# Four graph layers on one core: spline index blocks staged two ahead, rank picks half a block later, packed label products, aligned loops

## The reference

```python
# layer 0, twice: spline convolution, mean over incoming edges
msg = (1 - u) * (x @ w[0])[src] + u * (x @ w[1])[src]
h = segment_sum(msg, dst) / max(degree, 1) + x @ root + bias
# layer 1: opinion attention; edge_label is 8 wide, trans_weight 8 x 64
ef = edge_label @ trans_weight
att = sigmoid(leaky(x[row] * x[col] @ a) + leaky(ef @ edge_attention_weight))
# for values ef*att, x[col]*att, x[row]*att: segment sum, mean and max by row and by col
out = concat(...) @ weight + bias
# layer 2: three GCN convolutions; layer 3: softmax attention over incoming edges
```

## Time and profile before

| | us |
|---|---|
| median of three runs | 20658.94 |
| lowest, highest | 20649.24, 20679.84 |
| the profiled execution, its own time | 20593.66 |
| its span in the profile | 20591.8 |
| POOL busy | 12080.9 (59%) |
| DVE busy | 8998.8 (44%) |
| PE busy, its weight loads | 7375.4 (36%), 6283.1 |
| ACT busy | 2698.1 (13%) |

### The profile page before, as it was taken

How to read it: one execution, slowest core, us unless ns; L and a number is a source line. 1 busy time by engine, 2 the same in 40 slices (tenths; PEclk the granted TensorE clock), 3 DMA queues, 4 the chain that set the end, 5 groups by cost and what they waited for, 6 DMA issues and landing times. The chain is left out here.

```text
span 20591.8 us, 194797 instructions
## 1 busy us (share of the span) xinstructions
PE 7375.4 (36%) x49884; PEld 6283.1 (31%) x49884; DVE 8998.8 (44%) x25746; ACT 2698.1 (13%) x7499; POOL 12080.9 (59%) x11797
## 2 busy tenths in 40 slices
PE   3444444444322232232244544434444444400000
PEld 2333333333232232233211444434443333300000
DVE  3554533333343343344388444444443444333333
ACT  1222212222100000000023111111110111000000
POOL 4666656566566666666611466666665665466664
PEclk9655555555555555555555677767776666555555
DMA  1222212222122222222266000000000000022221
GB/s 56 62 62 62 63 58 80 80 82 84 59 86 81 79 83 84 79 82 81 82 222 234 8 11 12 11 11 11 12 11 19 22 21 21 15 55 56 57 56 42
DMA packets 599140, 1231.22 MB, mean 60 GB/s; under 512 B 229172, under 2 KB 351769, under 8 KB 572838
## 3 DMA queue, kind: packets, MB, share of 16 engines
q0 software_dynamic: 378560, 479.32, 10.7%
q1 hardware_dynamic: 206420, 692.77, 9.3%
q10 hardware_dynamic: 14112, 58.61, 0.8%
HBM read 560.63 MB, written 669.21 MB: 60 GB/s over the span
## 5 line engine op out<-in xcount | busy, mean ns | idle before, releaser
L795 POOL DMA_INDIRECT rows<-gcn_table,index x3430 | 3746.6, 1092 | 2491.0 <-ACT index L803 1509.6
L516 POOL DMA_INDIRECT rows<-spline_table,index x3136 | 3231.6, 1030 | 2038.5 <-ACT index L534 1077.5
L850 PE MATMUL p_slots<-part,lo_t 128*128 128x208 bf16 x18816 | 2549.3, 300 | 2920.8 <-ACT lo_t L812 1809.8
L850 PEld LDWEIGHTS p_slots<-part,lo_t 128*128 128x128 bf16 x18816 | 2007.1, 116 | 3346.1 <-issue 2369.6
L1036 POOL DMA_INDIRECT sent<-a_msg,a_place x1568 | 1578.1, 1006 | 1186.2 <-DVE a_run L1151 712.9
L1378 POOL DMA_INDIRECT e_rows<-soft_table,e_index x1568 | 1520.8, 970 | 845.3 <-issue 491.8
L1028 POOL DMA_INDIRECT a_rows<-att_table,a_index x1568 | 1506.5, 961 | 484.6 <-issue 470.4
L868 DVE TENSOR_TENSOR one_lo<-iota,lo 128x2560 bf16<-128x2560 f32 (+1 forms) x297 | 733.3, 2469 | 2315.5 <-ACT index L803 2125.4
L1092 PE MATMUL a_p_label<-tw,a_label 8*128 8x64 f32 x3136 | 1000.5, 401 | 2036.4 <-issue 1481.1
L1092 PEld LDWEIGHTS a_p_label<-tw,a_label 8*128 8x128 f32 x3136 | 853.2, 318 | 2014.7 <-issue 1728.4
L812 ACT ACTIVATE lo_t<-p_turn 128x512 bf16<-128x512 bf16 x1287 | 719.4, 595 | 5130.8 <-remote 3495.3
(11 more groups left out here) (398 smaller groups left out, 16071.2 us busy)
## 6 DMA issues: line engine op xcount, KB each, us to landing
running_dst<-a_run SPq DMA_DIRECT2D x98, 1600.0 KB
running_src<-s_run SPq DMA_DIRECT2D x98, 1600.0 KB
running<-e_run SPq DMA_DIRECT2D x98, 656.0 KB
s_rows<-sent ACTq DMA_DIRECT2D x98, 584.0 KB
rows<-gcn_table,index POOLq DMA_INDIRECT x3430
running<-run SPq DMA_DIRECT2D x98, 520.0 KB
rows<-spline_table,index POOLq DMA_INDIRECT x3136
running<-run SPq DMA_DIRECT2D x98, 512.0 KB
```

Source lines behind the costliest of these rows:

```text
L516: pool.indirect_dma_start(out=rows[h][:, k, :], out_offset=None, in_=table, in_offset=offsets(index[h][:, k:k + 1])).then_inc(gathered[h], 16)
L795: pool.indirect_dma_start(out=rows[h][:, ON_CHIP + k, :], out_offset=None, in_=table, in_offset=offsets(index[h][:, k:k + 1])).then_inc(ga ...
L850: ins = nc.tensor.matmul(p_slots[:, m, 0:CLASS * SLICE], lo_t[h][:, k, q, :], flat(part[:, c, q * CLASS:(q + 1) * CLASS, :]), start=q == 0 ...
```

## The change

It has three parts.

1. **Spline passes.** Indices are staged two halves ahead: ACT copies those of half n + 2 once the gathers of half n have landed, ahead of `stage` and the rank chain; the first two blocks are staged before the loop. POOL gets a wait for the messages of the half two back (step `MADE` = 2), since nothing else now keeps it from overwriting rows. Pick and reduction of half n − 1 move to half n, after the running chain and ahead of the one-hots; `p_look` is doubled for it. DVE's first iteration stands ahead of the loop, a memset counts two steps for the pick that is left out there, and the last pick follows the loop.
2. **Attention pass.** The labels are loaded packed: `a_label` is 128 partitions (16 columns × 8 labels) by 128 edges, 512 B a row of the DMA. PE makes one score product (16 columns wide) and two label products of 512 columns a half with the block-diagonal `w_labels`, in place of 32 small products. `tw_att` becomes the matching 128 × 16 block-diagonal vector, made once by a copy, a wider product and a reduction; the load of `tw` goes.
3. **Every pass, every engine:** `addr_align(256)` ahead of the loop puts its first instruction at a multiple of 256 in the engine's program, by empty instructions ahead of it.

```diff
@@ -483,11 +483,12 @@
...
             p_same = ctx.enter_context(nc.psum_tensor(f"p_same{uid}", [P, 12, P], F32))
-            p_look = ctx.enter_context(nc.psum_tensor(f"p_look{uid}", [P, RANKED, C], F32))
+            p_look = ctx.enter_context(nc.psum_tensor(f"p_look{uid}", [P, 2, RANKED, C], F32))
             turned, turned_sb, same, same_sb, summed, seen_sb, looked = (sem(n) for n in ("turned", "turned_sb", "same", "same_sb", "summed", "seen_sb", "looked"))
...
         running_v = running[0:EP, :].rearrange("(p t) c -> p t c", p=P)
-        INIT = per
+        INIT = 2 * per
+        MADE = 2
         Q = RANKED // GROUP
@@ -495,6 +496,7 @@
...
                 sp.dma_start(running[EP:EP + 1, cut], zeros[0:1, cut]).then_inc(stored[h], 16)
+            sp.addr_align(256)
             with sp.Fori(0, IT) as i:
@@ -507,10 +509,13 @@
...
         def _(pool):
+            pool.addr_align(256)
             with pool.Fori(0, IT) as i:
...
                     pool.wait_ge(indexed[h], i + 1)
+
+                    pool.wait_ge(stepped, INIT + per * (2 * i + h - 2) + MADE)
                     pool.sem_inc(sig["rounds"].sem, 1)
@@ -552,13 +557,15 @@
...
             stage_index(0, 0)
+            stage_index(1, B)
             stage(0, 0)
+            act.addr_align(256)
             with act.Fori(0, IT) as i:
...
-                    act.wait_ge(stepped, INIT + per * n - (per - 2))
-                    stage_index(1 - h, (n + 1) * B)
+                    act.wait_ge(gathered[h], 16 * B * (i + 1))
+                    stage_index(h, (n + 2) * B)
@@ -618,11 +625,12 @@
...
                             kk = q * GROUP + k
-                            nc.tensor.matmul(p_look[:, kk, 0:J], lo_tf[q % 2][:, k, :], seen[q % 2][:], start=True, stop=False)
+                            nc.tensor.matmul(p_look[:, h, kk, 0:J], lo_tf[q % 2][:, k, :], seen[q % 2][:], start=True, stop=False)
                             for j in range(k + 1):
-                                ins = nc.tensor.matmul(p_look[:, kk, 0:J], earlier[q % 2][:, PAIR[j] + k - j, :], one_hi[h][:, q * GROUP + j, :], start=False, stop=j == k)
+                                ins = nc.tensor.matmul(p_look[:, h, kk, 0:J], earlier[q % 2][:, PAIR[j] + k - j, :], one_hi[h][:, q * GROUP + j, :], start=False, stop=j == k)
                         ins.then_inc(looked, 1)
+                pe.addr_align(256)
                 with pe.Fori(0, IT) as i:
@@ -653,47 +661,68 @@
...
                 one_hots(0, lambda ins: ins.then_inc(stepped, 1))
-            with dve.Fori(0, IT) as i:
+            def pick(h, half, step):
+                dve.wait_ge(looked, Q * half)
+                step(nc.vector.tensor_tensor(picked[:], p_look[:, h, :, 0:J], one_hi[h][:], ALU.mult))
+
+            def rank_of(at, step):
+                step(nc.vector.tensor_reduce(edge["rank"][:, at], picked[:], AX.X, ALU.add))
+
+            def both_halves(i, first):
                 for h in range(2):
...
-                    def step(ins):
-                        ins.then_inc(stepped, 1)
-                        n[0] += 1
+                    def step(ins, by=1):
+                        ins.then_inc(stepped, by)
+                        n[0] += by
...
+                    half = 2 * i + h
                     dve.wait_ge(staged[h], i + 1)
...
                     step(nc.vector.tensor_tensor(msg[h][:, :, 0:C], msg[h][:, :, 0:C], rows[h][:, :, 0:C], ALU.add))
+                    assert n[0] == MADE
...
                         step(nc.vector.scalar_tensor_tensor(run[h][:, k, :], before, keep[h][:, k:k + 1], msg[h][:, k, :], ALU.mult, ALU.add))
+                    skipped = rank and first and h == 0
+                    if rank and not skipped:
+
+                        pick(1 - h, half, step)
+                        after()
+                        rank_of(bass.ds((half - 1) * B + ranked, RANKED), step)
                     if count or rank:
...
-                        dve.wait_ge(counted, 1 + B * (2 * i + h))
+                        dve.wait_ge(counted, 1 + B * half)
                     if count or rank:
                         one_hots(1 - h, step)
-                    if rank:
-
-                        dve.wait_ge(looked, Q * (2 * i + h + 1))
-                        step(nc.vector.tensor_tensor(picked[:], p_look[:, :, 0:J], one_hi[h][:], ALU.mult))
-                        after()
-                        step(nc.vector.tensor_reduce(edge["rank"][:, bass.ds((2 * i + h) * B + ranked, RANKED)], picked[:], AX.X, ALU.add))
+                    if skipped:
+                        step(nc.vector.memset(picked[:], 0.0), 2)
                     assert n[0] == per
-            dve.wait_ge(stepped, INIT + per * 2 * IT)
+            both_halves(0, True)
+            dve.addr_align(256)
+            with dve.Fori(1, IT) as i:
+                both_halves(i, False)
+            if rank:
+                done = lambda ins, by=1: ins.then_inc(stepped, by)
+                dve.wait_ge(stepped, INIT + per * 2 * IT)
+                pick(1, 2 * IT, done)
+                dve.wait_ge(stepped, INIT + per * 2 * IT + 1)
+                rank_of(slice((2 * IT - 1) * B + ranked, (2 * IT - 1) * B + B // 2 + ranked), done)
+            dve.wait_ge(stepped, INIT + per * 2 * IT + 2 * rank)
             nc.vector.tensor_copy(final[:, 0:width], run[1][:, B - 1, :]).then_inc(stepped, 1)
@@ -974,7 +1008,7 @@
...
         begun, xdst = pair("a_begun", [P, B, C]), pair("a_xdst", [P, B, C])
-        label, label_row = pair("a_label", [LABELS, B * P]), pair("a_label_row", [P, B, LABELS])
+        label, label_row = pair("a_label", [B * LABELS, P]), pair("a_label_row", [P, B, LABELS])
         product = sb("a_product", [P, B, C])
@@ -989,12 +1023,14 @@
...
         PLACED = 1 + B + 11
+        PRODUCTS = B * C // 512
...
                 sp.dma_start(begun[h][:], node_rows_v[:, bass.ds(n * B, B), :]).then_inc(loaded[h], 16)
-                sp.dma_start(label[h][:], labels[:, bass.ds(n * (B * P), B * P)]).then_inc(loaded[h], 16)
+                packed = labels[:, bass.ds(n * (B * P), B * P)].rearrange("l (k p) -> k l p", p=P)
+                sp.dma_start(label[h][:], packed).then_inc(loaded[h], 16)
                 sp.dma_start(label_row[h][:], label_rows[:, bass.ds(n * B, B), :]).then_inc(loaded[h], 16)
@@ -1081,16 +1120,17 @@
...
         def _(pe):
+            pe.addr_align(256)
             with pe.Fori(0, IT) as i:
...
                     pe.wait_ge(stepped, INIT + per * (2 * i + h - 1))
-                    for k in range(B):
-                        edges = label[h][:, k * P:(k + 1) * P]
-                        nc.tensor.matmul(p_label[h][:, k, :], edges, w_label, start=True, stop=True)
-                        ins = nc.tensor.matmul(p_score[h][:, k:k + 1], edges, w_label_att, start=True, stop=True)
+                    nc.tensor.matmul(p_score[h][:, 0:B], label[h][:], w_label_att, start=True, stop=True)
+                    for m in range(PRODUCTS):
+                        cut = slice(m * B // PRODUCTS, (m + 1) * B // PRODUCTS)
+                        ins = nc.tensor.matmul(flat(p_label[h][:, cut, :]), label[h][:], flat(w_labels[:, cut, :]), start=True, stop=True)
                     ins.then_inc(labelled, 1)
@@ -1654,7 +1704,7 @@
...
         w_ef, w_lab, twt = sb("w_ef", [C, 2, C]), sb("w_lab", [2 * LABELS, C]), sb("twt", [C, 3 * LABELS])
-        tw, ea, tw_att = sb("tw", [LABELS, C]), sb("ea", [C, 1]), sb("tw_att", [LABELS, 1])
+        ea, tw_att, tw_rows = sb("ea", [C, 1]), sb("tw_att", [B * LABELS, B]), sb("tw_rows", [C, B, LABELS])
         w_labels = sb("w_labels", [B * LABELS, B, C])
@@ -1665,7 +1715,7 @@
...
             (w_src[:], w_att[0:2 * C, :]), (w_dst[:], w_att[2 * C:4 * C, :]), (w_ef[:, 0, :], w_att[C:2 * C, :]), (w_ef[:, 1, :], w_att[3 * C:4 * C, :]),
-            (b1[:], bias1.broadcast_to([P, C])), (tw[:], trans), (twt[:, 0:LABELS], trans_t), (twt[:, LABELS:2 * LABELS], zeros[0:C, 0:LABELS]),
+            (b1[:], bias1.broadcast_to([P, C])), (twt[:, 0:LABELS], trans_t), (twt[:, LABELS:2 * LABELS], zeros[0:C, 0:LABELS]),
             (twt[:, 2 * LABELS:3 * LABELS], trans_t), (ea[:], edge_att), (att_b[:], att.broadcast_to([P, C])), (mix[:], agg_weights.broadcast_to([P, 3])),
@@ -1843,7 +1893,7 @@
...
-                    TABLE, SHIFTED, DEGREES = dve_s.base + 4, dve_s.base + 6, dve_s.base + 9
+                    TABLE, SHIFTED, DEGREES, MASKED = dve_s.base + 4, dve_s.base + 6, dve_s.base + 9, dve_s.base + 11
@@ -1854,7 +1904,8 @@
...
                     def _(pe):
-                        nc.tensor.matmul(ps[0:LABELS, 0:1], twt[:, 0:LABELS], ea[:], start=True, stop=True).then_inc(pe_s.sem, 1)
+                        pe.wait_ge(dve_s.sem, MASKED)
+                        nc.tensor.matmul(ps[:, 0:1], flat(tw_rows[:]), ea[:], start=True, stop=True).then_inc(pe_s.sem, 1)
@@ -1877,10 +1928,13 @@
...
                         assert step.n == DEGREES
```

(5 more changed lines are left out.)

22 lines of the change are left out of this document (20 added, 2 removed).

## The result

The changed kernel takes 21039.32 us (median of four, 21016.5 to 21050.96); the kernel before, 20667.22. The ratio is 1.0179, with a 95% interval of 1.0163 to 1.0196: 372 us slower. The forecast was 20194, the range 19600 to 20760. So the sign was wrong, and the result lies 279 us above the range.

A forecast was written before the change was run, and what follows sets the result against it. No engine fills the span; the order of waits bounds it, in the spline the PE/ACT chain with DVE's pick. −340 − 150 + 25 = −465 from the profiled 20593.7, plus 65.2: 20194 us, range 19600 to 20760.

The forecast's parts named there:

- the index two ahead: Spline passes: POOL waits for DVE's messages two halves back; alone worth 0, at most −744 us if the chain runs faster.
- The latency stays 23.7: Spline half of 25.1 us: with pick and reduction out of the loop, 23.7 us through PE and ACT remain.
- The −150: Spline passes, picks a half later: 1.2 and 0.35 us a half saved, 118 + 34 us over 98 halves each.
- Rival 3: Spline rank chain of PE: drawn-out issue if POOL's bursts join beyond 20 us; 6 us a half, 21520 us; chance 0.13.
- Against: Spline passes, objection to the slower case: DVE frees rows once a period, so a 3 us pause remains each half.
- three signs of being wrong: Spline iterations far from 48 to 50 us, DVE's run chain stepping by 1.40, queues q8 and q14 far from 48 packets.
- The deciding mark of 1.6 us a half: Spline passes: above this loss a half, 196 × x > 315, the spline loss outweighs the forecast's −340 and +25.
- −340: Attention, packed label products: iteration from 96.9 to 90 us, 6.9 × 49; ends 0 and −720.
- The walk: Attention iteration followed from 7521: pause shrinks to about 4 us, the next half runs slow; 88 to 92 us, 90 taken.
- +25: Alignment of loops: cost of POOL's empty slots at 8 starts, half the slots at an eighth of 0.20 us; bound 408.
- not fetched again: Alignment: instruction queues moved 48 packets in the whole run, so loop code is not refetched and aligning gains nothing.
- The other rule weighed: GpSimd touches only DVE instructions with two SBUF inputs, PE never waits; the slower spline case would then give about 20194.

The follow-up runs named there:

- e3: Kernel before with both spline edits (index two halves ahead, picks a half later), no alignment, late kind: 20827.07 us, ratio 1.0115.
- e4: Kernel before with the index staged two halves ahead alone, picks left in their half, late kind: 20845.98 us, ratio 1.0110.
- e14: Kernel before with picks and reductions a half later alone, index still one half ahead, late kind: 20757.51 us, ratio 1.0049.
- e15: Kernel before with both spline edits, POOL waiting for messages of the half just before, late kind: 20731.06 us, ratio 1.0030.
- e2: Kernel before with the packed label products of attention alone, late kind: 20533.97 us, ratio 0.9968.
- e1: Kernel before with only the 256 alignment ahead of all 24 loops, late kind: 20708.07 us, ratio 1.0049.
- e13: Changed kernel with the counts' semaphore raised once a half instead of 16 times, late kind: 20995.04 us, ratio 1.0160 against the kernel before.
- e5: Changed kernel with the counts' semaphore raised once a half instead of 16 times, prompt kind: 17401.06 us, ratio 1.0042 against the kernel before.

## Why the prediction was wrong

**The step that failed** is this one, under the index two ahead: "POOL then leads by one gather burst, but rows are freed once per period, so its pause stays, 3 us a half, unless the chain shortens. Alone worth 0". Rows are freed once a half, but POOL, which now finds two blocks free, joins them to a run of 42.6 us (median) where it had 21.7, and the pause comes once, 15 us long. I took each half's pause for an average, not for the thing that releases the chain. With it fell "The latency stays 23.7": that latency was never a property of PE and ACT. It held 8.5 us of late release in the rows I had read the earlier trace rows, and on a prompt chip the whole half takes 21.8. Rows are freed so that POOL need not stop, and it was its stopping that let the others go on. The −150 became +273 and +38 in the profiled execution; e3 puts the edits alone at +224 (the medians) and e4 and e14 show that either of them loses. e15 takes most of it away again (1.0030 for 1.0115) by making POOL wait each half.

**Rival 3 came nearest**, with chance 0.13: its place (the rank chain) and its condition (bursts joined beyond 20 us) were met in the first pass, and its "Against" (a pause remains each half) is what failed. Its mechanism was not the right one. It has PE's instructions spaced out; in the changed kernel PE's look products stand 98 us where they stood 621 (300 to 2600 us), of which 36 and 244 without a releaser, and DVE's chain in the same stretch stands 46 us over 1302 steps. What stands is ACT and DVE, for releases, and ACT was said to be untouched. So it had the sign right by a cause beside the true one. Its price was too high: 6 us a half supposed, 2.8 measured in the first pass (273 / 98), 0.4 in the second, where POOL's runs stay 20.2 us. Of the three signs of being wrong two were met, iterations of 57.7 us and 90 packets; the third, a chain of DVE at 1.40 us a step, was not. The deciding mark of 1.6 us a half was met as a mean (311 / 196 = 1.6), and only because the next term failed did the total come out clearly slower.

**Attention: −340 taken, +22 measured, about none beside a like chip (4736 us for 4736 and 4734 in e14 and e15), −67 alone.** DVE's wait went as forecast (10.8 us a half to 0.1), the products shrank as forecast. The mechanism of the limit was right ("a POOL that never pauses keeps DVE slow" stands there as drawn out), the size off by a factor of five: 6.9 us an iteration for 1.4 (67 / 49). The walk was done for one iteration with its end quick; e2 shows three bursts joined, 123.8 us, before a pause of 20.7. It should have been read as a budget: POOL stands 559 us in e2 between 5900 and 10100 us where it stood 629, so only 70 of that came back.

**Alignment: +25 taken, +105 measured (e1)**, 48 packets read as "not fetched again". That was right for the turns of the loop and blind for its start: the packets rose to 90, and at the start of the source pass some come only after POOL's gathers. That start costs 76 us, of which the pass gives 44 back. The +25 itself, the price of empty slots, was an estimate that no run shows. The rule of the Trainium skill, Runtime: NRT & Kernel Launch, section Instruction fetch mechanics, by which a stall would be saved at each turn, got no clear support. On the late kind the source pass is quicker with alignment each time (800.5 us here, 802.3 in e1, 800.6 in e13, for 846.2, 847.0 in e2 and 846.1 in e14); on the prompt kind it takes 800 to 804 either way. But in the kernel before no code packet falls between 10400.2 and 11255.0 us, which is nearly all of that pass, so a fetch at each turn is not what was saved there. What was stays open.

**The sum by the medians:** alignment +105, attention −69, spline +224 make 260; the change costs 372. About 110 us are interaction. In the profiles it shows in two places: with alignment and packed products together attention is 4736 for 4647 with the products alone and 4726 with alignment alone, and the spline passes are 2741 and 2560 for 2689 and 2516 in e3. Part of both may be the other chip. I can't name its cause.

The other rule weighed, that of the Trainium skill, SBUF — State Buffer, section Who interferes with whom, would have left this case at 20194. (It lets GpSimd touch DVE's instructions in the two-port modes too, which the prediction leaves out.) PE and ACT stood all the same, 1443 us before ACT's lo_t, but for semaphores and on one kind of chip alone; the rule is about ports, and no run here tests it there.

## What to carry to other kernels

When a chain through several engines stands beside a queue of indirect DMAs, look at when the late releases end, not only at who releases: if they end a few us after POOL stops, POOL's pauses are part of the chain, and freeing POOL takes them away. A wait removed there can come back on the next step of the chain; count what the engines must do between two pauses. And before such a kernel is tuned by 1%, run it on more than one chip: 16% of its time existed on one kind only, and each of the edits that ran on both has another price there (the picks 1.0028 and 1.0049, POOL held to one block 1.0526 and 1.0030, the change with one count signal 1.004 and 1.016).

## What was not expected of the hardware

- The same program took 20603 to 20667 us on some chips and 17326 on others, with like durations of gathers (1071 and 1059 ns in the first spline pass). What differed is the time from the end of an instruction to its release elsewhere: lo_t stood 489.0 us in 181 times on the one (first pass, kernel before), 1.6 in 199 on the other.
- Where releases are late, they are late in POOL's runs of indirect DMAs. The long ones end 4.6 us after the last gather (1006.70 to 1011.31), shorter ones within the run. In the first pass, runs of 42.6 us cost lo_t 8.8 us a copy (1443.0 / 164), runs of 21.7 with breaks of some 4 us 2.7 (489.0 / 181), runs of 21.8 with breaks of 5 us nothing (e15), but runs of 67 us only 3.6 (e4): the length of the runs is not the whole rule.
- On that kind the fetch of code at a loop start came after POOL's gathers as well: 76.58 us in e13 against 14.39 in e5, the same program. Chained instructions of DVE 1.40 us apart and this may have one cause; that was not shown.
